# Linear attention with a routed feed-forward, one core: VectorE's transposes of the first pass read runs of 32 columns, and the weights are laid out for it first

## The reference, cut to what matters

```python
# x: (1, 8192, 512) fp32, E = 512, 16 heads of 32
sa, ca, ga, sb, cb, gb = split(silu(c) @ wmod)          # six rows of 512
h  = layernorm(x) * (1 + ca) + sa
q  = elu(h @ Wq.T + bq) + 1;  k = elu(h @ Wk.T + bk) + 1;  v = h @ Wv.T + bv
KV = sum_s k[s] v[s]  (per head);   Z = 1 / (q . sum_s k[s] + 1e-6)
x  = x + ga * ((q KV Z) @ Wo.T + bo)
h  = layernorm(x) * (1 + cb) + sb
x  = x + gb * routed_ffn(h)                              # 8 experts of 32, two chosen per row
```

## Time and profile before

| | |
|---|---|
| median of 3 runs | 1313.26 us (1312.13 to 1314.66) |
| the profiled execution | 1314.87 us, span 1312.8 us |
| granted clock of TensorE, mean | 0.988 |
| PE busy | 1239.4 us, 94% |
| DVE busy | 1023.9 us, 78% |
| ACT, POOL busy | 545.8 us, 42%; 558.3 us, 43% |
| first pass | about 25 to 640 us |

### The profile page before, as it was taken

One profiled execution on the slowest core, in us unless ns is written; L12 is line 12 of the kernel. 1 busy time (PEld: TensorE's weight loads), 2 busy tenths in 40 slices (PEclk: granted clock), 3 DMA queues, 4 the chain that ended last, 5 costly groups with the idle time before them and its releaser, 6 DMA issues.

```text
span 1312.8 us, 18763 instructions
## 1 busy us (share of the span) xinstructions
PE 1239.4 (94%) x5846; PEld 1015.6 (77%) x5846; DVE 1023.9 (78%) x2259; ACT 545.8 (42%) x1125; POOL 558.3 (43%) x397
## 2 busy tenths in 40 slices
PE   8888989899999999999779999999999999999998
PEld 7666767678888888888568888878888888888887
DVE  6788887888878778777767778777778787787764
ACT  2433444355555554555234344343343343433431
POOL 1322223344444444443346455455464454554631
PEclk8989999999999999999899999999999999999999
DMA  6665322344433333342312231231321322313201
GB/s 208 189 194 144 96 89 89 97 129 129 127 125 126 122 124 124 121 128 97 104 49 69 77 97 58 88 97 49 97 82 63 97 68 77 97 56 90 81 17 49
DMA packets 138130, 131.92 MB, mean 100 GB/s; under 512 B 26680, under 2 KB 91320, under 8 KB 138032
## 3 DMA queue, kind: packets, MB, share of 16 engines
q1 hardware_dynamic: 138032, 130.73, 32.4%
HBM read 80.88 MB, written 49.81 MB: 100 GB/s over the span
## 4 chain that ended last, share of the span: by engine, by line
PE 54%; POOL 15%; issue 14%; DVE 7%; ACT 2%; DMA 1%; POOLq 0%; SPq 0%; ACTq 0%; DVEq 0%
PE ps L1434 17%; PE ps L1435 17%; PE ps L1439 17%; POOL xb L629 6%; POOL rrs L668 3%; PE ps L1645 2%; POOL xn_lo L621 2%; POOL rstd L661 2%; DVE x L1262 2%; DVE xT_lo L1269 1%; POOL ks_acc L617 1%; DVE marked L1352 1%; ACT xn L830 1%; POOL rstd L612 1%; DVE m L1345 1%
## 5 line engine op out<-in xcount | busy, mean ns | idle before, releaser
L655 POOL TENSOR_TENSOR cn<-c,half 128x16 f32<-128x16 f32 x32 | 104.1, 3254 | 281.6 <-DVE c L1297 281.6
L617 POOL TENSOR_TENSOR ks_acc<-ks_acc,zk 128x512 f32<-128x512 f32 x64 | 83.1, 1299 | 151.8 <-DVE zk L1170 151.8
L612 POOL TENSOR_TENSOR rstd<-veps,neg_half 128x1 f32<-128x1 f32 x64 | 35.1, 549 | 238.3 <-DVE veps L899 238.3
L1434 PE MATMUL ps<-wk_hi,xT_hi 128*128 128x512 f32 x256 | 103.5, 404 | 13.5 <-ACT xT_hi L731 11.6
L621 POOL TENSOR_TENSOR xn_lo<-xn,xn_hi 128x512 fp32r<-128x512 f32 x64 | 110.9, 1733 | 6.6 <-ACT xn_hi L766 6.6
L1434 PE MATMUL ps<-g_hi,qT_hi 128*128 128x512 f32 x256 | 104.8, 409 | 7.7 <-ACT qT_hi L794 7.7
L1434 PE MATMUL ps<-wq_hi,xT_hi 128*128 128x512 f32 x256 | 103.6, 405 | 1.3 <-DVE zq L1143 1.3
L1434 PE MATMUL ps<-k_hi,xn_hi 128*128 128x512 f32 x256 | 103.8, 405 | 0.0
L1434 PE MATMUL ps<-v_hi,xT_hi 128*128 128x512 f32 x256 | 102.9, 402 | 0.0
L1435 PE MATMUL ps<-wk_lo,xT_hi 128*128 128x512 f32 x256 | 102.1, 399 | 0.0
L1435 PE MATMUL ps<-k_lo,xn_hi 128*128 128x512 f32 x256 | 102.0, 398 | 0.0
(11 more groups left out here) (246 smaller groups left out, 3392.5 us busy)
## 6 DMA issues: line engine op xcount, KB each, us to landing
xin<-_attn_hidden_states_dram SPq DMA_DIRECT2D x64, 256.0 KB, 3.0
q_scratch<-qf SPq DMA_DIRECT2D x64, 256.0 KB, 3.2
xin<-_attn_hidden_states_dram SPq DMA_DIRECT2D x32, 512.0 KB, 4.0
q_in<-q_scratch SPq DMA_DIRECT2D x128, 128.0 KB, 2.9
out_dram<-qf SPq DMA_DIRECT2D x64, 256.0 KB, 2.0
xn_scratch<-xn SPq DMA_DIRECT2D x62, 256.0 KB, 2.1
xq<-xn_scratch SPq DMA_DIRECT2D x248, 64.0 KB, 2.5
wm_in<-in_L_wmod_dram SPq DMA_DIRECT2D x4, 1024.0 KB, 5.4
```

What stands on the lines that cost most here:

```text
L612: nc.gpsimd.tensor_tensor(rstd[:, s:s + 1], veps[:, s:s + 1], neg_half[:, 0:1], ALU.pow).then_inc(rstd_done, 1)
L617: nc.gpsimd.tensor_tensor(ks_acc[:], ks_acc[:], kf[:, s, :], ALU.add).then_inc(ks_done, 1)
L655: nc.gpsimd.tensor_tensor(cn[:].rearrange("p h e -> p (h e)"), c2[:].rearrange("p h e -> p (h e)"), half[:], ALU.pow).then_inc(cn_done, 1)
L1434: nc.tensor.matmul(dst, ah, bh, start=start and n == 0, stop=False)
```

## The change

`turned_x` reads runs of 32 columns, so block j of the transposed tile holds features 128c + 32j + f on partition 32c + f. Everything that meets it is laid out the same way: ScalarE copies `raw_k` into four buffers (`k_turn`: both halves of `exp_k` and `zk`, not yet in use) and `mod1` into `mod1p`, GpSimd copies `raw_q` (`q_turn`) and, for the later job `sc`, `mod1` into `wtmp`, and also lays out tiles 0 and 1 in `xq`. TensorE then reads whole runs of 128 columns. Its order of jobs changes: k0 to k3 come ahead of `sa`. The table `PREP` stays as it is.

```diff
+MOD2_LOADS = {-1: 0, 1: 1, 3: 2, 5: 3}
...
-        JOBS = ["sa", "k0", "k1", "k2", "k3", "q0", "q1", "q2", "q3"]
-        BANK = dict(zip(JOBS, (0, 4, 2, 3, 1, 6, 7, 5, 0)))
+        JOBS = ["k0", "k1", "k2", "k3", "sa", "q0", "q1", "q2", "q3"]
+        BANK = dict(zip(JOBS, (4, 2, 3, 1, 0, 6, 7, 5, 0)))
...
+        k_turn = [exp_k[:, 0, :], exp_k[:, 1, :], zk[:, 0, :], zk[:, 1, :]]
+        q_turn = [exp_q[:, 0, :], exp_q[:, 1, :], zq[:, 0, :], zq[:, 1, :]]
+
+        mod1p = mod2[:, 2:4, :]
+
+        def quads(raw, b):
+
+            return raw[:].rearrange("p r (i j d) -> p r i j d", i=KB, j=KB)[:, :, :, b, :]
+
+        def in_quads(buf):
+
+            return buf.rearrange("p (r i d) -> p r i d", r=KB, i=KB)
...
@@ SyncE, loads(i)
-                if i in (-1, 1, 3, 5):
-                    v = (i + 1) // 2
+                if i in MOD2_LOADS:
+                    v = MOD2_LOADS[i]
...
@@ GpSimd, step(i, s) of the first pass
+                if -1 <= i <= 0:
+                    pool.wait_ge(xn_done, i + 2)
+                    nc.gpsimd.tensor_copy(xq[:, 1 - s, :].rearrange("p (j i d) -> p i j d", i=KB, j=KB),
+                                          xn[:, 1 - s, :].rearrange("p (i j d) -> p i j d", i=KB, j=KB)).then_inc(xp_done, 1)
                 if live(i + 2, T):
                     wait_count(pool, veps_done, i + 3)
                     nc.gpsimd.tensor_tensor(rstd[:, s:s + 1], veps[:, s:s + 1], neg_half[:, 0:1],
                                             ALU.pow).then_inc(rstd_done, 1)
+                if i == -1:
+                    pool.wait_ge(wq_in, 16)
+                    for b in range(KB):
+                        nc.gpsimd.tensor_copy(in_quads(q_turn[b]), quads(raw_q, b)).then_inc(pq_done, 1)
+                    pool.wait_ge(mod1_done, KB)
+                    nc.gpsimd.tensor_copy(wtmp[:], mod1[:]).then_inc(mod1n_done, 1)
...
@@ ScalarE, ahead of hi_scaled("k0")
+            act.wait_ge(wk_in, 16)
+            for b in range(KB):
+                nc.scalar.copy(in_quads(k_turn[b]), quads(raw_k, b)).then_inc(pk_done, 1)
+            act.wait_ge(mod1_done, KB)
+            for v in (1, 0):
+                nc.scalar.copy(mod1p[:, v, :].rearrange("p (j i d) -> p i j d", i=KB, j=KB),
+                               mod1[:, v, :].rearrange("p (i j d) -> p i j d", i=KB, j=KB)).then_inc(mod1p_done, 1)
...
@@ VectorE, turned_x(i, s)
                 nc.vector.transpose(bank_xT.rearrange("p (j g t) -> p g j t", j=KB, g=KB),
-                                    xq[:, s, :].rearrange("p (g f j) -> p g j f", g=KB, j=KB)).then_inc(xTb_done, 1)
+                                    xq[:, s, :].rearrange("p (g j f) -> p g j f", g=KB, j=KB)).then_inc(xTb_done, 1)
...
@@ VectorE, b2_and_value_bias
+                dve.wait_ge(mod2_done, 4 * KB)
...
@@ TensorE
-            pe.wait_ge(mod1_done, KB)
-            strided_columns("sa", 0, mod1[:, 0, :])
-            strided_columns("sa", KB, mod1[:, 1, :]).then_inc(prep_psum, 1)
-            pe.wait_ge(wk_in, 16)
             for b in range(KB):
-                transposes(f"k{b}", every_fourth(raw_k, b))
-            pe.wait_ge(wq_in, 16)
+                pe.wait_ge(pk_done, b + 1)
+                transposes(f"k{b}", [k_turn[b][:, r * P:(r + 1) * P] for r in range(KB)])
+            pe.wait_ge(mod1p_done, 2)
+            columns("sa", 0, [(mod1p[:, 0, :], all_rows)])
+            columns("sa", KB, [(mod1p[:, 1, :], all_rows)]).then_inc(prep_psum, 1)
             for b in range(KB):
-                transposes(f"q{b}", every_fourth(raw_q, b))
+                pe.wait_ge(pq_done, b + 1)
+                transposes(f"q{b}", [q_turn[b][:, r * P:(r + 1) * P] for r in range(KB)])
...
@@ TensorE, prepare, job "sc"
+                        pe.wait_ge(mod1n_done, 1)
-                        columns(j, 0, [(mod1[:, 0, :], all_rows)])
-                        columns(j, KB, [(mod1[:, 1, :], all_rows)]).then_inc(prep_psum, 1)
+                        columns(j, 0, [(wtmp[:, 0, :], all_rows)])
+                        columns(j, KB, [(wtmp[:, 1, :], all_rows)]).then_inc(prep_psum, 1)
...
@@ TensorE, step(i, s)
                 if isinstance(i, int) and i <= 0:
-                    pe.wait_ge(xn_done, i + 2)
+                    pe.wait_ge(xp_done, i + 2)
                     if i == -1:
                         pe.wait_ge(acc_step, SUMMED["k0"] + 1)
                     wait_count(pe, xTl_done, i + 1)
                     for b in range(KB):
-                        last = nc.tensor.transpose(bank_xT[:, b * P:(b + 1) * P], xn[:, 1 - s, b::KB], ident[:])
+                        last = nc.tensor.transpose(bank_xT[:, b * P:(b + 1) * P], xq[:, 1 - s, b * P:(b + 1) * P], ident[:])
```

More of the change, by code:

```diff
@@ L280, in build @@
         wq_in = sem("wq_in")
+        pk_done = sem("pk_done")
+        pq_done = sem("pq_done")
+        mod1n_done = sem("mod1n_done")
+        mod1p_done = sem("mod1p_done")
+        xp_done = sem("xp_done")
         wma_in = [sem(f"wma_in{b}") for b in range(KB)]
@@ L452, in bank_free @@
                 eng.wait_ge(acc_step, SUMMED[before[-1]] + 1)
-        HI_JOBS = ["k0", "k1", "k2", "k3", "q0", "q1", "q2", "q3",
-                   "fv0", "fv1", "fv2", "fv3", "u0", "u1", "u2", "u3", "w20", "w21", "g0", "g1", "g2", "g3"]
+        HI_JOBS = (["k0", "k1", "k2", "k3", "q0", "q1", "q2", "q3"]
+                   + [j for j in JOBS if j[:2] in ("fv", "w2") or j[0] == "u"] + ["g0", "g1", "g2", "g3"])
         HI = {j: n for n, j in enumerate(HI_JOBS)}
@@ L1183, in step @@
                 prepare(i, 2)
-                if isinstance(i, int) and i == 16:
+                if i == 16:
                     b2_and_value_bias()
@@ L1449, in transposes @@
                 last.then_inc(prep_psum, 1)
-            def every_fourth(raw, fb):
-                return [raw[:, r, fb::KB] for r in range(KB)]
             def blocks_of(raw, fb):
@@ L1476, in _ @@
             all_rows, first_row = ones[:, 0:1], ident[:, 0:1]
[L1477 to L1481, removed]
-            pe.wait_ge(mod1_done, KB)
-            strided_columns("sa", 0, mod1[:, 0, :])
-            strided_columns("sa", KB, mod1[:, 1, :]).then_inc(prep_psum, 1)
-            pe.wait_ge(wk_in, 16)
-            for b in range(KB):
-                transposes(f"k{b}", every_fourth(raw_k, b))
-            pe.wait_ge(wq_in, 16)
+            for b in range(KB):
+                pe.wait_ge(pk_done, b + 1)
[3 more added lines that the diff above has]
+            columns("sa", KB, [(mod1p[:, 1, :], all_rows)]).then_inc(prep_psum, 1)
             for b in range(KB):
-                transposes(f"q{b}", every_fourth(raw_q, b))
+                pe.wait_ge(pq_done, b + 1)
+                transposes(f"q{b}", [q_turn[b][:, r * P:(r + 1) * P] for r in range(KB)])
             SUMS = {"ga": 0, "gb": 3}
```

## The result

The changed kernel takes 1317.79 us, the median of 20 runs (1314.25 to 1322.19). The kernel before took 1314.05 in the same sessions (20 runs, 1312.11 to 1316.81). The ratio is 1.0029 with a 95% interval of 1.0019 to 1.0038: slower by 0.29%, some 3.8 us. The forecast was 0.3 us less than before; the time lies inside the range, but on the slow side of no change.

What follows compares the result with a forecast made beforehand. VectorE's queue was taken to bound the kernel from 46 to 276 us, TensorE afterwards. A start 7.1 us later less 7.4 us gained by transposes gave 1313.26 - 0.3 = 1313.0 us, range 1309 to 1319.

Steps and rivals of the forecast that it cites:

- What bounds the kernel: First pass: VectorE's queue sets the pace from 46 to 276 us, TensorE afterwards and in the second pass.
- The transposes: First-pass VectorE transposes (L915): 0.41 us saved each, bounds 0 and 0.49; 18 count between 46 and 276 us.
- the sum: Whole kernel: 7.1 us lost at the start less 7.4 gained by transposes, giving 1313.0 us; this case's chance 0.36.
- no gain, 0.07: Rival, first-pass transposes: the PSUM write sets their rate, 0 gained, 7.1 us lost, 1320.4 us; chance 0.07.
- pays throughout: Rival, all 62 transposes: a faster VectorE gains 25 us, less 7, giving 1295 us; chance 0.01.
- The start: Before 46 us: ScalarE and GpSimd copies come first, so bk_row and every later VectorE instruction is 7.1 us late.
- the clock stays low: Rival, first products: TensorE's lower clock costs 1.6 to 4.7 us, time 1314.6 to 1317.7; chance 0.28.
- SyncE issues the same transfers in the same order; each waits for a signal that comes as late as VectorE does, so they move along: SyncE's transfer queue after the start: transfers shift along with VectorE, at no cost.
- The term of the sum that was mis-sized: Transposes for tiles 2 to 21, 46 to 276 us: 18 x 0.41 = 7.4 us gained, at most 9.8, at least 0.
- New VectorE waits for TensorE in steps 7 to 15: Sign of error, first pass: the forecast is wrong if VectorE runs into such waits; no size given.
- slower had 0.30: Whole kernel, chance of slower: 0.15 low clock, 0.08 dear copy, and the transposes without gain.
- slow cases: Rivals: low clock 1314.6 to 1317.7 us (0.28), dear GpSimd copies 1315 (0.10), transposes without gain 1320.4 (0.07).

Runs made afterwards that it cites:

- e1: Kernel before with only the read pattern of the first pass's VectorE transposes changed to runs of 32 (products wrong): 1310.85 us, 0.9967.
- e13: The changed kernel once more, unaltered, in another session: 1317.85 us, 1.0015 of the kernel before.
- e3: The changed kernel with Wo's 16 transfers issued four at a time in steps 2 to 5: 1314.84 us, 0.9999 of the kernel before.
- e12: e1 with Wo's 16 transfers spread over steps 2 to 5 (products wrong): 0.9951 of the kernel before.
- e6: e5 with Wo's 16 transfers spread over steps 2 to 5: 1307.44 us, 0.9930 of the kernel before.
- e5: Changed kernel, GpSimd's raw_q copies ahead of rstd, tile 1's layout ahead of xn_lo, mod1 layout and sums sa ahead of k: 1309.8 us, 0.9958.
- e7: The kernel before with Wo's 16 transfers spread over steps 2 to 5: 0.9995 of the kernel before.
- e8: The changed kernel with 16 idle-time matmuls of 128 columns ahead of bv's sums in step 5: 1319.64 us, 1.0027 of the kernel before.
- e11: e6 with 20 idle-time matmuls of 128 columns behind the g products, between the passes: 1310.25 us, 0.9957 of the kernel before.
- e10: The kernel before with 20 idle-time matmuls of 128 columns between the passes: 1.0004 of the kernel before.

## Why the prediction was wrong

- **What bounds the kernel** was read rightly: VectorE's queue to about 276 us, TensorE afterwards (343.00 of 343 busy, again 8.37 us per tile).
- **The transposes** were right in kind and near in size: 0.385 us saved instead of 0.41. In the term of the sum, 18 x 0.385 = 6.9 instead of 7.4. e1 changed the read alone, with the write into PSUM as it was, and the 0.385 us came. The Trainium skill, "SBUF — State Buffer", Specifications, asks for two hits in a 16-byte line for full bandwidth, which makes the read the slow part; by that rule, e1 agrees. That rival (no gain, 0.07) is out, and so is "pays throughout" (0.01).
- **The start** was right in its sum (6.75 against 7.1) and wrong in its terms. `sa_col` was 2.4 us late, not 4.65: ScalarE's copies began 0.8 us earlier than forecast, and the 16 sums ran at the upper level (1.84 us, as in the earlier trace rows) instead of mostly at the lower. GpSimd's four copies of `raw_q` took 0.58 us each (1.16 for two), next to the memset's 0.52, not 0.9, and that of `mod1` 1.04, not 1.8. The forecast left GpSimd idle for 0.8 us before `xn_lo`; it stood idle for 3.15, until `xn_hi`, which gave part of this back. So TensorE's transposes of tile 1 stand at 29.67, 2.5 us before the forecast's 32.2. The other way went the first product: 4.73 us for 12 matmuls, where 12 x 0.232 = 2.8 was reckoned, since the lower clock lasted to 34.5. That is 2 us, the rival "the clock stays low" in part. 7.1 - 2.5 + 2.0 = 6.6. The Trainium skill's 0.77 us for an unrolled loop over 512 elements ("GPSIMD Engine Reference", section 3.1) is above what the copy took here too, and the measurement decides.
- **The step that failed** is this sentence: "SyncE issues the same transfers in the same order; each waits for a signal that comes as late as VectorE does, so they move along". They did not. The queue fell behind at `bv_row` and in tile 4's round trip, and behind the 16 of `raw_o`, which hold it for 10.66 us in before and after alike, it had no time to catch up: tile 5's `xq` came 8.7 us later than in before, with VectorE only some 5.6 late, and VectorE waited for it, 2.19 us in after and 1.65 in e13. The margin of 0.9 us could be read from the trace of before and was not computed. With Wo spread over four steps the wait is gone and the changed kernel gives 0.9999; without it 1.0029 and 1.0015. e3, e12 against e1, and e6 against e5 all point that way, with e7 as the control. The wait itself is some 2 us; how much of the rest comes of the late tile is open.
- **The term of the sum that was mis-sized** is the gain: e1 measures 4.3 us where 7.4 stood. The forecast lost two of twenty transposes to waits for TensorE. In e1 these waits grow by 3.7 us (`zq` by 2.2, `wtmp` new with 1.5), the late tile takes 0.6, and some 2.4 us go between the passes, where the forecast had nothing change.
- **"New VectorE waits for TensorE in steps 7 to 15"** was named as a sign of error. They came earlier, in steps 5 and 6 (`bias_cols` 1.68, `zq` 2.38), and once later for ScalarE (`wtmp`, 1.5). In after they stand right behind the late tile; but in e6 and e12 `zq` waits as long (2.39 and 2.35 us) without one, so a faster VectorE can meet TensorE there anyway. So the rival that the forecast named only as a sign is part of the answer. How much of it the clock makes is not settled.
- **The chances**: slower had 0.30. None of the rivals was the queue; the prices that had been put on slow cases came out near the measured time by another mechanism.

## What to carry to other kernels

When a change makes one engine later or faster, work out the margin of every transfer that it will ask for, above all of those behind a burst in the same DMA queue: 16 issues held the queue for 10.66 us, and the tile behind them had 0.9 us to spare in one trace and none in another. A burst that nobody needs at once belongs spread over steps; alone it was worth nothing (e7), with the change 0.16 to 0.3%. New work at the start goes into the queue where the engine would wait: with the same copies, the order alone was worth 0.6 to 0.7% (e5's 0.9958 against the two measurements of after).

## What the runs showed of the hardware

- A GpSimd copy of 512 fp32 columns in runs of 32 took 0.58 us in the trace of after, one of 1024 columns in a row 1.04, so the runs cost it little; but the one of 512 at 6.58 us, beside VectorE's scaling of `wm_in`, took 1.06.
- VectorE's transpose of 512 fp32 columns takes 720 ns with reads in runs of 32, 1105 with every fourth float. The write into PSUM is the same in both (e1 against before), so the stride is what costs.
- An idle-time fp32 matmul of 128 columns shows as two instructions of some 0.115 us (e8: 16 asked for, 32 in 3.73 us).
- Work placed in TensorE's wait between the passes moved the stretches at the lower clock (in e6 they begin at 631.1, 641.4 and 655.0, in e11 at 657.7 and 678.2); in before it bought no time (e10, 1.0004 [0.9994, 1.0014]).
- Two executions of one kernel, after and e13, differ by 3.1 us at step 22.
